# Expert results scattered into token order, read back as plain blocks, with the expert weight loads on another queue

## The chip, the cores and the metric

The kernel runs on one core of a Trainium2 chip. The metric is the time of one execution on the device, in microseconds (us). Five engines run their own instruction streams and meet through semaphores: TensorE (PE; PEld is its weight load), VectorE (DVE), ScalarE (ACT), GpSimd (POOL), and SyncE (SP), which here only issues DMAs. PEq, POOLq and so on are the sequencers of the engines. ACT and POOL can issue DMAs too.

## What is computed

Two transformer layers on x of shape 4 x 1024 x 256, in float32. Layer 0 adds causal attention and a dense feed-forward to x. Layer 1 adds a gated attention and a mixture of 8 experts, both on the same normalized rows:

```python
xn = _layernorm(x, axis=-1)
x = x + _L0_attn_ref(xn, ...) + _L0_ffn_ref(xn, ...)
xn = _layernorm(x, axis=-1)
x = x + _L1_attn_ref(xn, ...) + _L1_ffn_ref(xn, ...)

# _L1_ffn_ref, with E = 8 experts, K = 2 per token
scores = jax.nn.softmax(xf @ Wg.T, axis=-1)
expert_weights, expert_indices = jax.lax.top_k(scores, K)
expert_weights = expert_weights / expert_weights.sum(-1, keepdims=True)
gates = (jax.nn.one_hot(expert_indices, E) * expert_weights[..., None]).sum(axis=1)
g = jax.nn.silu(_lora_in(xf, W1, b1, A1, B1)) * _lora_in(xf, W3, b3, A3, B3)
y_e = _lora_out(g, W2, b2, A2, B2)
y = jnp.einsum('te,ted->td', gates, y_e)
```

## The kernel before

The program has four stages, and each engine runs through them in a fixed order written out as lists of units (`LAYER0_UNITS`, `ATTENTION_UNITS`, `TURN`, and `experts_order`). Near a stage's end a few units of the next one are put in between (`AHEAD`). In this text a unit is named by its letters and number.

Stage 0 (to about 480 us) is layer 0 for all four batches. It also folds the low-rank parts into the expert weights and writes these to DRAM, and it routes. For each token and each of its two choices, POOL writes a row of 257 floats (the normalized token and its gate) to a slot of `slot_rows_scratch` with an indirect DMA (`SC`, line 576, 64 of them). The slots of one expert lie together, so that 71 tiles of 128 rows are left, each of one expert.

Stage 1 (to about 592 us) is layer 1's attention for the first two batches. DVE computes the tables of tiles and experts here (`TB:0` to `TB:6`), and with `TB:7` (nine instructions) the row at which each token's two results will stand (`result_rows`). POOL loads the first expert in the unit `LE`.

Stage 2 (about 592 to 945 us) is the experts: 71 turns of 4.9 us, one for a tile. In turn j the units on PE and DVE are `MA(j+2)`, `MG(j+1)`, `MR(j+3)`, `MC(j+2)`, `MO(j)`. `MR` transposes the rows of a tile, `MA` and `MC` multiply them by two matrices, `MG` transposes the gated product and `MO` multiplies it by the third matrix. ACT does `MG(j+1)`, `MR(j+3)` (copies from PSUM, line 2130) and `MA(j+2)`, which is the SiLU (line 2143). DVE makes `slots_g` from the SiLU's output (line 2182), which `MG` on PE waits for, and the results `ys_ring` (line 2190, a ring of 4). SP's unit `MT(j)` waits for the results of tile j, then loads the slot rows of tile j+6 into `xs_ring` (line 2011, a ring of 6) and stores the results in slot order, as a plain block (line 2012). POOL loads the weights of experts 1 to 7: `ME` (two of three parts and their bias, when the last hidden products of the expert that had the ring slot are read) and `MB` (the third, later). `MU` on SP, at turn 12, loads the rows that stage 3 starts with.

Stage 3 (from 945 us) is the attention for the last two batches. Its results, and those of the first half, are added up in SBUF. To each of 32 tiles of 128 tokens POOL adds the two expert results: 64 indirect DMAs that gather 128 rows and add them (`GX0`, `GX1` for the second half, `GZ0`, `GZ1` for the first; line 1485). Between them POOL computes `rsy`, the power -0.5 of the variances (`YS`, line 1495), for which the final rows (`YF`, lines 1849 and 1857) wait on DVE. SP stores the finished blocks: `SZ` for the first half (line 1473), `SX` for the second (line 1454, and tile by tile at the end, line 1451).

`QK` of stage 3 on ACT writes `q` and `r` (lines 1715 to 1717), which lie in the same memory as `xs_ring`.

## Time and profile before

| | us |
|---|---|
| median of 3 runs | 1084.84 (1083.53 to 1085.21) |
| the profiled execution, its own time | 1088.44 |
| its span, first to last instruction | 1086.8 |
| PE busy | 1044.9 (96%) |
| DVE busy | 798.4 (73%) |
| POOL busy | 432.9 (40%) |
| ACT busy | 393.8 (36%) |
| mean granted clock of PE | 0.981 of full speed |

Busy times are the durations of an engine's instructions. Matmuls overlap in the pipeline, and their ends are modelled. A time from issue to landing is that from the start of a DMA's instruction to the last packet's completion.

### The profile page before, as it was taken

Reading aid. Unit: us, or ns where it says so; the run is one execution under the profiler, and the core shown is the slowest. Engines: PE = TensorE matmul, PEld = TensorE weight load, DVE = VectorE, ACT = ScalarE, POOL = GpSimd, SP = SyncE. Lnnn points to the kernel's source line nnn. Section 1 sums busy time; section 2 is a strip of 40 time slices with the busy share of each in tenths; the row PEclk is TensorE's granted clock in tenths of the full one; section 3 lists DMA queues with packets and bytes.
Section 4 is the critical chain, followed back from the end, with each engine's and each line's share of the span. In section 5 each row is a group of like instructions: output and inputs, shape, how many; then the busy total and the mean of one; then the engine's idle time right before and its main releaser. Section 6 shows DMA issues by size and latency. Waiting matters only on the chain.

```text
span 1086.8 us, 20552 instructions
## 1 busy us (share of the span) xinstructions
PE 1044.9 (96%) x6154; PEld 896.6 (83%) x6154; DVE 798.4 (73%) x1842; ACT 393.8 (36%) x794; POOL 432.9 (40%) x408
## 2 busy tenths in 40 slices
PE   5999999999999999989999999999999999999995
PEld 4899888888989798967868788888888888867774
DVE  5667987798788877786866777777777777763745
ACT  2544454445443536352410222232323232352300
POOL 2723666566656565254112110101001000088886
PEclk7999999999999999989999999999999999999998
DMA  8333344544454436331055556424355151265556
GB/s 253 106 114 120 128 163 140 187 147 141 147 176 145 143 113 226 106 101 50 6 159 171 189 179 210 155 97 148 113 180 195 56 197 50 75 140 86 75 101 146
DMA packets 87255, 147.69 MB, mean 136 GB/s; under 512 B 8433, under 2 KB 64625, under 8 KB 87025
## 3 DMA queue, kind: packets, MB, share of 16 engines
q1 hardware_dynamic: 66416, 98.11, 27.8%
q0 software_dynamic: 20736, 48.28, 16.2%
q8 instruction: 57, 0.93, 0.4%
q14 instruction: 46, 0.37, 0.1%
HBM read 88.91 MB, written 57.45 MB: 135 GB/s over the span
## 4 chain that ended last, share of the span: by engine, by line
PE 68%; DVE 14%; POOL 6%; issue 6%; DMA 4%; ACT 1%; DVEq 0%; POOLq 0%; SPq 0%; ACTq 0%
PE wide L2072 19%; PE wide L592 11%; PE bank L592 11%; PE bank L2072 9%; PE wide L1553 3%; PE bank L2097 3%; POOL first_half L1485 3%; DVE hT L1022 2%; PE wide L1646 2%; DMA x_second<-slot_results_scratch,result_rows 2%; POOL x1b L1485 2%; PE bank L2065 1%; PE bank L1622 1%; POOL x_second L1485 1%; PE bank L1553 1%
## 5 line engine op out<-in xcount | busy, mean ns | idle before, releaser
L2130 ACT ACTIVATE gsT<-bank 128x512 fp32r<-128x512 f32 x71 | 42.5, 599 | 243.4 <-PE bank L2097 243.4
L1945 POOL DMA_DIRECT2D expert_ring<-experts_scratch x24 | 17.1, 711 | 253.3 <-DVE slots_h L2179 186.1
L2072 PEld LDWEIGHTS wide<-expert_ring,gsT 128*128 128x128 f32 x852 | 112.1, 189 | 6.6 <-issue 0.3
L2072 PE MATMUL wide<-expert_ring,xsT 128*128 x432 | 115.9, 404 | 0.9 <-DVE xsT L2161 0.8
L2072 PE MATMUL wide<-expert_ring,gsT 128*128 x852 | 114.0, 282 | 0.1
L2072 PE MATMUL bank<-expert_ring,xsT 128*128 x420 | 112.8, 403 | 0.5 <-issue 0.5
L2072 PEld LDWEIGHTS wide<-expert_ring,xsT 128*128 128x128 f32 x432 | 76.1, 188 | 15.1 <-issue 1.8
L563 POOL TENSOR_TENSOR folded_matrix<-fold,folded_matrix 128x512 fp32r<-128x512 f32 x48 | 64.5, 1350 | 59.7 <-ACT folded_matrix L778 59.6
L576 POOL DMA_INDIRECT slot_rows_scratch<-u,slot x64 | 66.5, 1039 | 49.9 <-issue 20.6
L2072 PEld LDWEIGHTS bank<-expert_ring,xsT 128*128 128x128 f32 x420 | 74.0, 188 | 14.1 <-issue 1.1
L592 PE MATMUL bank<-w,hT 128*128 128x264 f32 x480 | 61.5, 285 | 0.5 <-DVE hT L1022 0.5
L592 PEld LDWEIGHTS bank<-w,hT 128*128 128x128 f32 x480 | 59.5, 188 | 0.8 <-issue 0.7
L592 PE MATMUL wide<-xnT,pT 128*128 128x512 f32 (+2 forms) x288 | 58.8, 350 | 0.0
L1485 POOL DMA_INDIRECT x1b<-slot_results_scratch,result_rows x16 | 27.5, 1721 | 73.4 <-DVE x1b L1813 68.9
L1022 DVE TENSOR_TENSOR hT<-hid,hT 128x512 fp32r<-128x512 f32 x64 | 54.7, 861 | 2.5 <-ACT hid L834 2.3
L2161 DVE TENSOR_TENSOR gsT<-bank,gsT 128x512 fp32r<-128x512 f32 x71 | 49.0, 690 | 9.5 <-ACT gsT L2130 1.4
L2182 DVE SCALAR_TENSOR_TENSOR slots_g<-slots_h,xs_ring,slots_h 128x512 f32<-128x512 f32 x71 | 53.4, 752 | 2.5
L1485 POOL DMA_INDIRECT first_half<-slot_results_scratch,result_rows x32 | 51.5, 1610 | 9.3 <-issue 9.0
L2173 DVE TENSOR_TENSOR slots_h<-wide,expert_bias 128x512 f32<-128x512 f32 x36 | 24.9, 692 | 39.5 <-PE wide L2072 39.5
L592 PEld LDWEIGHTS wide<-xnT,pT 128*128 128x128 f32 x288 | 47.9, 188 | 6.5 <-ACT xp L815 0.3
L592 PE MATMUL bank<-xnT,w 128*128 128x512 f32 x192 | 52.5, 417 | 0.0
L592 PE MATMUL wide<-xnT,w 128*128 128x512 f32 x192 | 49.7, 399 | 0.0
(322 smaller groups left out, 2481.9 us busy)
## 6 DMA issues: line engine op xcount, KB each, us to landing
experts_scratch<-folded_matrix SPq DMA_DIRECT2D x24, 1024.0 KB, 5.2
expert_ring<-experts_scratch POOLq DMA_DIRECT2D x24, 1024.0 KB, 5.5
raw<-in_expert_weights SPq DMA_DIRECT2D x24, 512.0 KB, 6.2
xs_ring<-slot_rows_scratch SPq DMA_DIRECT2D x71, 128.5 KB, 2.5
slot_results_scratch<-ys_ring SPq DMA_DIRECT2D x71, 128.0 KB, 2.6
lora<-in_expert_lora SPq DMA_DIRECT2D x24, 288.0 KB, 3.2
u<-in_L_attn_x SPq DMA_DIRECT2D x4, 1024.0 KB, 5.5
expert_bias<-in_expert_bias POOLq DMA_DIRECT2D x8, 512.0 KB, 6.9
```

The source lines that it names most:

```text
L563: tt(fold_part(n, 1), fold[:, n % 2, :], fold_part(n, 0), ALU.subtract).then_inc(matrix_ready, 1)
L576: nc.gpsimd.indirect_dma_start(out=scr["xs"], in_=xb[:, b % 2, t, 0:ROW], in_offset=None, bounds_check=SLOTS - 1, out_offset=bass.Indirect ...
L592: ins = mm(o, stationary(i), moving(j), start=(first and q == 0), stop=(last and q == 2))
L1022: tt(hT[:, 1, n % IC, :], hid[:, n % 2, :], hT[:, 0, n % IC, :], ALU.subtract).then_inc(hid_low, 1)
L1485: nc.gpsimd.indirect_dma_start(out=target, out_offset=None, in_=scr["ys"], in_offset=index(k, tile_at), bounds_check=SLOTS_T * P - 1, comp ...
L1553: ins = mm(o, stationary(i), moving(j), start=(first and k == 0), stop=(last and k == 2))
L2072: ins = mm(o, parts[i], moving, start=(first and q == 0), stop=(last and q == 2))
L2097: ins = tr(T[1][:, c * P:(c + 1) * P], g[:, j % 2, c * P:(c + 1) * P], ident[:])
L2130: return nc.scalar.activation(o, i, ACT.Copy)
L2161: tt(flat[1], bank, flat[0], ALU.subtract).then_inc(taken, 1)
L2173: tt(h1[:, j % 2, :], H[j % 2][0], bias(e, 0, HID), ALU.add).then_inc(h1_ready, 1)
L2182: stt(out=g[:, i, :], in0=h1[:, i, :], scalar=xs[:, j % ROUND, DIM:ROW], in1=h3[:, i, :], op0=ALU.mult, op1=ALU.mult).then_inc(g_ready, 1)
```

## The change

The results of a tile go to DRAM in token order. The slot row gets a second extra column, `PLACE`, with the row in `token_results_scratch` (2 x 4096 rows) to which the result belongs. DVE writes it in stage 0, with one small instruction for each batch and choice. POOL stores each tile's results with an indirect DMA that takes its row numbers from `xs_ring`: 71 of them instead of 71 plain stores by SP. Because `xs_ring` is now read until that store is done, the next rows may be loaded only after its completion; `xs_ring` has 7 places instead of 6. SP loads the rows of the first 7 tiles, ACT those of the other 64, in the new unit `ML(j+5)` between `MR(j+3)` and `MA(j+2)`. It first waits until the results of tile j-2 have been stored. `QK` of stage 3 on ACT waits until all results are stored.

SP loads the experts' weights. `MU` is moved from turn 12 to just behind the arrival of expert 1. Spare slots get an index out of bounds (the float 1.0 read as an integer), so that nothing is written for them.

In stage 3 the sums are made by 16 plain DMAs with addition, each of 4 tiles (512 KB), instead of 64 indirect ones of one tile. `TB:7` and `result_rows` are gone.

```diff
-ROUND = 6
+ROUND = 7
-ROW = DIM + 1
+ROW = DIM + 2
+PLACE = DIM + 1
...
+            def places(k):
+                ts(x[:, :, PLACE].bitcast(I32), keep["token_at"][:], float(k * TOKENS + OF[b] * SEQ), None, ALU.add)
...
+                places(0)
                 nc.vector.reciprocal(x[:, :, DIM], gate1[:]).then_inc(g_step, 1)
...
     "gpsimd": """
-        ZR:0 ZR:1 ZR:2 ZR:3 ZR:4 YS:1 ZR:5 YS:3 ZR:6 YS:5 ZR:7 YS:7 YS:9 LE:0 LE:1 YS:11 LE:2 YS:13 YS:15
+        ZR:0 ZR:1 ZR:2 ZR:3 ZR:4 YS:1 ZR:5 YS:3 ZR:6 YS:5 ZR:7 YS:7 YS:9 YS:11 YS:13 YS:15
     "sync": """
-        LC:0 LC:1 LC:3 LX:0 LC:2 SX:0 CL:0 SX:1 LX:1 SX:2 SX:3
+        LC:0 LC:1 LC:3 LX:0 LC:2 SX:0 CL:0 SX:1 LX:1 LE:0 LE:1 LE:2 SX:2 SX:3
...
-    "sync": "CL:0:1 SX:1:1 LX:1:5 SX:2:4",
+    "sync": "LX:1:7 SX:2:1",
...
     if engine == "sync":
-        first = [("ML", j) for j in range(ROUND)]
-        return first + [u for j in range(SLOTS_T) for u in ([("MU", 0)] if j == 2 * ROUND else []) + [("MT", j)]]
+        loads = [("MB", 0), ("ME", 1), ("MB", 1), ("MU", 0)]
+        return [("ML", j) for j in range(ROUND)] + loads + [u for e in range(2, E) for u in (("ME", e), ("MB", e))]
     if engine == "gpsimd":
-        return [("MB", 0)] + [u for e in range(1, E) for u in (("ME", e), ("MB", e))]
+        return [("MT", j) for j in range(SLOTS_T)]
     if engine == "scalar":
-        every = (("MG", 1), ("MR", 3), ("MA", 2))
+        every = (("MG", 1), ("MR", 3), ("ML", ROUND - 2), ("MA", 2))
...
+        def add_rows(target, k, b, rows_of, name, n):
+            if k:
+                pool.wait_ge(added[name][n], 16)
+            nc.gpsimd.dma_start(out=target, in_=results[k, b][:, rows_of, :], accum_op=ALU.add).then_inc(added[name][n], 16)
...
             elif kind == "QK":
+                if half and n == 0:
+                    before["results_stored"](act)
...
+            kind, j = un
+            pool.wait_ge(y_taken, j + 1)
+            nc.gpsimd.indirect_dma_start(
+                out=scr["ys"], in_=y[:, j % RING, :], in_offset=None, bounds_check=TOPK * TOKENS - 1, oob_is_err=False,
+                out_offset=bass.IndirectOffsetOnAxis(ap=xs[:, j % ROUND, PLACE:ROW].bitcast(I32), axis=0)
+                ).then_inc(y_out[j % RING], 16)
...
+        def next_rows(j):
+            done = j - ROUND
+            act.wait_ge(y_out[done % RING], 16 * (done // RING + 1))
+            row_load(act, j)
```

On ACT, in the middle of stage 2, this is what stands in a turn and the start of the next before. `gsT` is `MG`, `xsT` is `MR`, and `slots_h` is the SiLU of `MA`:

```order
L2130 ACTIVATE gsT<-bank 128x512 [waits gated_transposed]
L2130 ACTIVATE xsT<-bank 128x256 [waits slots_transposed]
L2143 ACTIVATE slots_h_112<-slots_h_112 128x512 [waits h1_biased]
L2130 ACTIVATE gsT<-bank 128x512 [waits gated_transposed]
L2130 ACTIVATE xsT<-bank 128x256 [waits slots_transposed]
```

And in a turn now, on the same engine at the same place; `slots_out2` is the semaphore of a finished store of results, and `TENSOR_LOAD` reads the tile's place from SBUF into a register:

```order
L2126 ACTIVATE gsT<-bank 128x512 [waits gated_transposed]
L2126 ACTIVATE xsT<-bank 128x256 [waits slots_transposed]
L1988 TENSOR_LOAD tile_row [waits slots_out2]
L1988 ISA x2
L1993 ISA
L1993 DMA xs_ring<-slot_rows_scratch 128x258
L2139 ACTIVATE slots_h_111<-slots_h_111 128x512 [waits h1_biased]
```

The load of the slot rows has moved to ACT, and its wait stands between two ACT instructions of the turn.

On ACT, at the start of stage 3, the first instruction on `q` stands like this before:

```order
L1673 ACTIVATE u<-u,r 128x256 [waits l1_u_in]
L1673 ACTIVATE u<-u,r 128x256
L1720 ACTIVATE v_52<-v_52 128x512 [waits attention_g_taken2]
L1715 ACTIVATE q<-bank,cols_79 128x512 [waits attention_g_done]
L1716 ACTIVATE r<-bank,cols_79 64x512
```

And now:

```order
L1676 ACTIVATE u<-u,r 128x256 [waits l1_u_in]
L1676 ACTIVATE u<-u,r 128x256
L1725 ACTIVATE v_52<-v_52 128x512 [waits attention_g_taken2]
L1720 ACTIVATE q<-bank,cols_79 128x512 [waits slots_out3,slots_out2,attention_g_done,slots_out1,slots_out0]
L1721 ACTIVATE r<-bank,cols_79 64x512
```

The order is the same; `q` has four more semaphores to wait for, those of the stores of results.

On SP, where stage 1 goes over into stage 2, this stands before, around a store of the first half's rows (`attention_x_ready` is the semaphore of these rows):

```order
L1996 TENSOR_LOAD tile_row [waits expert_out_taken]
L1996 ISA x2
L2011 ISA
L2011 DMA xs_ring<-slot_rows_scratch 128x257
L2012 DMA slot_results_scratch<-ys_ring 128x256
L1454 DMA x_scratch<-x1b 128x4x256 [waits attention_x_ready]
```

Now it is this (the row loads of 7 tiles stand ahead of the first row; `attention_g_done` is the semaphore of PE's products):

```order
L1930 TENSOR_LOAD rank_expert [waits matrix_out,ranks_ready]
L1930 ISA x2
L1938 ISA
L1938 DMA expert_ring<-experts_scratch 128x2x1024
...
L1462 DMA x_scratch<-x1b 128x4x256 [waits attention_x_ready]
L1462 DMA x_scratch<-x1b 128x4x256 [waits expert_in0_0,expert_in0_1,expert_in0_2,attention_x_ready]
L1930 TENSOR_LOAD rank_expert [waits attention_g_done]
...
L1322 DMA u<-xn_scratch 128x8x256 [waits expert_in1_0,expert_in1_1,expert_in1_2]
```

Where the store of the last rows of the first half stood beside the experts' results before, the load of expert 1 (line 1930 and what follows) now stands behind it on SP, and `MU` (line 1322) behind the arrival of expert 1.

## Rows read from the trace of the kernel before

**Rows 1.** The head of the page.

```profile
span 1086.8 us, 20552 instructions
```

**Rows 2.** Busy time by stretch: length, PE, PEld, DVE, ACT, POOL, PEclk, DMA share, GB/s.

```profile
680.00:720.00 40.00, 40.00 (x248) 35.22 (x247) 29.28 (x49) 11.24 (x24) 3.22 (x5) 1.00 0.45 149
```

**Rows 3.** Timeline of the end: start, length, instruction, [idle before and what ended it].

```profile
1077.80 1.57 POOL L1485 DMA_INDIRECT first_half<-slot_results_scratch,result_rows  x1 [0.30 <-issue]
1078.91 1.21 POOL L1495 TENSOR_TENSOR rsy<-vey,half 128x2 f32<-128x2 f32 x1
1080.15 0.88 DVE L1849 SCALAR_TENSOR_TENSOR y<-y,mvy,ln_w 128x256 f32<-128x256 f32 x2 [1.33 <-POOL rsy L1495]
1080.95 0.88 DVE L1857 SCALAR_TENSOR_TENSOR x_second<-y,rsy,x_second 128x256 f32<-128x256 f32 x2
1081.77 0.37 SPq L1473 DMA_DIRECT2D out_dram<-first_half  x1
```

**Rows 4.** The final stores: length min/median/max in ns, first and last start.

```profile
L1451 SPq DMA_DIRECT2D out_dram<-x_second x4: 452/480/944, 1082.2 to 1084.2; - x4
```

**Rows 5.** Timeline of one turn of stage 2.

```profile
931.65 0.48 DVE L2190 SCALAR_TENSOR_TENSOR ys_ring<-expert_bias,xs_ring,wide 128x256 f32<-128x256 f32 x1
...
933.88 0.38 ACT L2130 ACTIVATE xsT<-bank 128x256 fp32r<-128x256 f32 x1
...
934.14 0.63 ACT L2143 ACTIVATE slots_h<-slots_h 128x512 f32<-128x512 f32 x1
...
935.85 0.75 DVE L2182 SCALAR_TENSOR_TENSOR slots_g<-slots_h,xs_ring,slots_h 128x512 f32<-128x512 f32 x1
...
937.65 0.60 PE L2097 MATMUL bank<-ident,slots_g 128*128 128x128 f32 x4
```

**Rows 6.** SP's row loads, the register read and the first six DMAs.

```profile
L1996 SPq TENSOR_LOAD <-tile_row x71: 263/268/477, 555.7 to 922.3; - x71
```
```profile
L2007 SPq DMA_DIRECT2D xs_ring<-slot_rows_scratch x6: 338/354/360, 556.7 to 572.4; - x6
```

**Rows 7.** Indirect stores of stage 0: releaser, one at 183.5 us, its landing, all landings.

```profile
L1075 DVE COPY u<-second_gate x4: 165/169/1149, 182.5 to 482.5; 128x8 f32<-128x8 f32 x4
```
```profile
L576 POOL DMA_INDIRECT slot_rows_scratch<-u,slot x1: 1049/1049/1049, 183.5 to 183.5; - x1
...
DMA to landing us min/median/max: 6.1/6.1/6.1
```
```profile
DMA to landing us min/median/max: 2.4/2.8/6.6
```

**Rows 8.** SP at the same time.

```profile
180.89 0.55 SPq L483 DMA_DIRECT2D experts_scratch<-folded_matrix  x1
```

**Rows 9.** An expert load, SP's store beside it, and that store's landing.

```profile
637.24 0.70 POOL L1945 DMA_DIRECT2D expert_ring<-experts_scratch  x1 [27.32 <-DVE slots_h L2179]
```
```profile
638.86 0.75 SPq L2012 DMA_DIRECT2D slot_results_scratch<-ys_ring  x1
```
```profile
slot_results_scratch<-ys_ring SPq DMA_DIRECT2D x1, 128.0 KB, 8.2
```

**Rows 10.** Timeline, DVE where stage 1 ends.

```profile
618.88 0.88 DVE L1857 SCALAR_TENSOR_TENSOR x1b<-y,rsy,x1b 128x256 f32<-128x256 f32 x2
```

**Rows 11.** Timeline of the first microseconds of stage 3.

```profile
945.33 0.48 DVE L2190 SCALAR_TENSOR_TENSOR ys_ring<-expert_bias,xs_ring,wide 128x256 f32<-128x256 f32 x1 [0.69 <-PE wide L2072]
...
946.41 0.99 SPq L1463 DMA_DIRECT2D first_half<-x_scratch  x2
...
952.51 0.69 ACT L1715 ACTIVATE q<-bank,cols 128x512 f32<-128x512 f32 x1
...
959.70 0.66 PE L1582 MATMUL bank<-ident,headB 128*128 128x128 f32 x4 [0.87 <-DVE headB L1802]
```

**Rows 12.** A wait of PE in stage 1, and the stretch behind it.

```profile
479.23 0.82 PE L1582 MATMUL bank<-ident,headB 128*128 128x128 f32 x4 [2.02 <-DVE headB L1802]
```
```profile
480.00:482.00 2.00, 2.00 (x10) 1.78 (x9) 1.85 (x4) 1.11 (x2) 0.05 (x1) 0.50 0.19 66
```

More of the change, by code:

```diff
@@ L234, in tile_rooms @@
     keep["bv"], keep["bo"], keep["cols1"] = a.take("bv", [P, H1]), a.take("bo", [P, DIM]), a.take("cols1", [P, 17])
-    keep["result"] = a.take("result_rows", [P, TOPK, TILES], I32)
     a = Room(nc, *chain)
@@ L1074, in unit @@
                 hold(dve, v_held, *rows_moved(b, 0))
+                places(1)
                 nc.vector.tensor_copy(x[:, :, DIM], gate1[:]).then_inc(gates_turned, 1)
@@ L1370, in attention @@
     x1_b = scr["x1"].rearrange("(b t p) d -> b p t d", p=P, t=TPB)
+    results = scr["ys"].rearrange("(k b t p) d -> k b p t d", k=TOPK, p=P, t=TPB)
     def t_use(un):
@@ L1997, in rows_of, with row_load, arrived, loaded @@
         return rows[bass.ds(at, 1)].rearrange("s p d -> (s p) d")
+    def row_load(engine, j):
+        engine.dma_start(xs[:, j % ROUND, :], rows_of(engine, xs_d, j)).then_inc(x_in[j % ROUND], 16)
     def sync(sp):
+        def arrived(e, m):
+            sp.wait_ge(keep["expert_in"][e % 2][m], PARTS_IN[m] * (e // 2 + 1))
+            sp.sem_inc(expert_ready[m], 1)
+        def loaded(e, parts, left=None):
+            of = expert_of_rank(sp, keep, e)
+            if e >= 2:
+                end = sp.value_load(keep["rank_end"][0:1, e - 2:e - 1], min_val=0, max_val=SLOTS_T)
+                sp.wait_ge(left, end)
+            for m in parts:
+                load_expert_part(sp, io, keep, scr, e, m, of)
         def unit(un):
@@ L2005, in unit @@
                     sp.wait_ge(*before["heads_done"])
-                    sp.wait_ge(keep["ranks_ready"], 4)
-                sp.dma_start(xs[:, j % ROUND, :], rows_of(sp, xs_d, j)).then_inc(x_in[j % ROUND], 16)
-            elif kind == "MT":
-                sp.wait_ge(y_taken, j + 1)
-                if j + ROUND < SLOTS_T:
-                    sp.dma_start(xs[:, j % ROUND, :], rows_of(sp, xs_d, j + ROUND)).then_inc(x_in[j % ROUND], 16)
-                sp.dma_start(ys_d[j], y[:, j % RING, :]).then_inc(y_out[j % RING], 16)
+                    sp.wait_ge(keep["ranks_ready"], 3)
+                row_load(sp, j)
+            elif kind == "ME" and j == 1:
+                sp.wait_ge(*before["output_done"])
+                loaded(j, range(3))
+            elif kind == "ME":
+                loaded(j, (0, 1), h_taken)
+            elif kind == "MB":
+                for m in (0, 1):
+                    arrived(j, m)
+                if j >= 2:
+                    loaded(j, (2,), y_taken)
+                arrived(j, 2)
             elif kind == "MU":
@@ L2022, in gpsimd @@
     def gpsimd(pool):
-        def arrived(e, m):
-            pool.wait_ge(keep["expert_in"][e % 2][m], PARTS_IN[m] * (e // 2 + 1))
-            pool.sem_inc(expert_ready[m], 1)
-        def loaded(e, parts, left=None):
-            of = expert_of_rank(pool, keep, e)
-            if e >= 2:
-                end = pool.value_load(keep["rank_end"][0:1, e - 2:e - 1], min_val=0, max_val=SLOTS_T)
-                hold(pool, loader_held, left, end)
-            for m in parts:
-                load_expert_part(pool, io, keep, scr, e, m, of)
-        def unit(un):
-            kind, e = un
-            if kind == "ME" and e == 1:
-                hold(pool, loader_held, *before["output_done"])
-                loaded(e, range(3))
-            elif kind == "ME":
-                loaded(e, (0, 1), h_taken)
-            elif kind == "MB":
-                for m in (0, 1):
-                    arrived(e, m)
-                if e >= 2:
-                    loaded(e, (2,), y_taken)
-                arrived(e, 2)
+        def unit(un):
+            kind, j = un
[4 more added lines that the diff above has]
+                ).then_inc(y_out[j % RING], 16)
         return unit
@@ L2181, in gate @@
             dve.wait_ge(s_ready, s + 1)
-            stt(out=g[:, i, :], in0=h1[:, i, :], scalar=xs[:, j % ROUND, DIM:ROW], in1=h3[:, i, :], op0=ALU.mult, op1=ALU.mult
+            stt(out=g[:, i, :], in0=h1[:, i, :], scalar=xs[:, j % ROUND, DIM:PLACE], in1=h3[:, i, :], op0=ALU.mult, op1=ALU.mult
                 ).then_inc(g_ready, 1)
```

102 lines of the change are left out of this document (41 added, 61 removed).

## The prediction, made before the changed kernel was run

> **What bounds the kernel now.** I read the head of the page first [rows 1]: 1086.8 us from first to last instruction, in an execution that took 1088.44 us. The sum below is a difference in this execution, and I carry it over to the median of the runs, 1084.84 us, unchanged. Then the busy times by stretch. In the middle of the experts' stage PE is busy for all of a stretch of 40 us at full clock [rows 2], and so it is in the five that follow. So stage 2 is PE's, 4.91 us for a tile, and no work taken from SP, POOL or DVE there can shorten it. The change can win only where PE waits or has ended, and it loses wherever it makes PE wait. Last I read the timelines of the seams, where other engines hand over to PE, and of the end.
>
> **The end: what it gains.** The last `rsy` on POOL is shown from 1078.91, but the indirect gather before it runs from 1077.80 to 1079.37, so it can run only from there to 1080.12 and takes about 0.75 us; DVE waited 1.33 us for it [rows 3]. Now no gather stands ahead of it on POOL (the last addition stands ahead of the last three `rsy`), so it ends at about 1079.67: 0.45 us earlier. DVE's last rows are then done at 1081.83 - 0.45 = 1081.4. SP's gain is larger. The store of the first half's last block was issued only at 1081.77, since it waited for that last gather, and the four stores of the second half stood behind it, from 1082.2 to 1084.2 for the last [rows 3, 4]. With the additions done long before, the first stores go out when their rows are ready, and the last one right behind DVE's last instruction, at 1081.4. The end moves from 1084.2 to 1081.4: **-2.8 us**. If `rsy` is no faster it is -2.3; if earlier waits for `rsy` (0.4 us each, of the same kind) go too, -3.6. What hides the 16 larger additions is some 100 us of stage 3 between them and their readers. POOL is less busy than with 64 gathers, and the one block that is needed last is issued between two `rsy` well before its reader.
>
> **Edits with one answer.** `TB:7` goes from DVE in a stretch in which PE doesn't wait: 0. Eight small instructions write the places; one like them takes 0.17 us [rows 7]. One stands ahead of the head that PE waits 2.02 us for [rows 12]: +0.2 at most, and I take **+0.2**. POOL's share of the loads moves to SP, whose issues cost no engine anything. The first expert's loads stand behind 7 row loads on SP, but the six row loads of before had ended at 572.4 [rows 6], and stage 2 begins at 592: 0. One more small constant is loaded at the start: 0.
>
> **The middle: a new wait on ACT.** In a turn ACT copies `xsT` at 933.88 and starts the SiLU at 934.14; DVE makes `slots_g` of it at 935.85, and PE takes that at 937.65 [rows 5]. Between copy and SiLU ACT now waits for the store of the results of two tiles ago, reads a register and issues a DMA. On SP the way from the register read to the DMA is 1.0 us (555.7 to 556.7), and the DMA's issue 0.35 [rows 6]. Without any wait the SiLU thus starts near 935.3 and ends near 936.0, and `slots_g` ends near 936.8, still 0.9 us before PE wants it. So the 64 register reads and issues cost nothing. They use up 1.2 of the 2.1 us of cover, though. What is left decides on the wait. For PE not to wait, `slots_g` must start by 936.65, the SiLU by 935.97, the DMA by 935.55, the register read by 934.5. The results that it waits for are those of two turns before; their instruction ended at 931.65 + 0.48 - 4.91 = 927.2. The store has **7.3 us** from the end of the result instruction to its completion. Behind ACT's wait are queued the SiLU, then the next turn's copies for PE. DVE's `slots_g` waits for it, and PE's `MG` for that.
>
> How long does it take? No indirect store of results is in the trace of before, but two neighbours are. The 64 indirect stores of slot rows are of the same size: 2.4 to 6.6 us from issue, 2.8 as a rule, and POOL starts one about 0.8 us after DVE's releasing instruction (182.5 + 0.17 to 183.5) [rows 7]. So as a rule 3.6 us, and no wait. But the one at 183.5 us took 6.1, while 2 MB of SP's transfers, begun at 180.89, were in flight [rows 7, 8]: 6.9 us after its releaser. The second neighbour is SP's own store. At each change of expert 2.5 MB are loaded, here from 637.24 [rows 9]. The store issued at 638.86 landed 8.2 us later. By the turn of 4.91 us its results were ready at 637.83, so it was done **9.2 us** after them. It is the first of six such switches (experts 2 to 7), and nobody waited for it. Now ACT does. SP reacts half a microsecond faster than POOL and so starts the bulk earlier; I take 8.6 us, and 8.6 - 7.3 = 1.3 us that PE waits. Ends: 3.6 us is no wait, 10.0 (9.2 plus POOL's slower start) is 2.7. For experts 3 to 7 that is 5 x 1.3 = **+6.5 us** (0 to 13.5).
>
> **The opening of stage 2.** Expert 1 now stands on SP behind the store of the first half's last rows, which are ready at 618.88 + 0.88 = 619.8 [rows 10]; before, POOL loaded it some 13 us earlier, when no result store had a reader. So 3.6 MB begin near 620 beside the stores of the first tiles, which ACT waits for. When they have arrived, `MU` adds 3 MB, and expert 2 comes on top of that. 8.2 us was the price of 2.5 MB; with more in flight I take 2.5 us for the first collision and 2 for those with `MU` and expert 2: **+4.5 us** (0 to 9).
>
> **The start of stage 3.** `QK` on ACT ran at 952.51, and the head that comes of it is what PE waited for (0.87 us at 959.70) [rows 11]. So this is a chain with no cover behind it. It now waits for the last store of results. Those are ready at 945.81; SP begins 3 MB of loads at 946.41, POOL's store starts near 946.6 and has its packets ready a microsecond later. At 8.6 us after the results it is done at 954.4, and a little more for 3 MB is 955: **+2.5 us** (0, if it is done in 3.6, to 6).
>
> **The clock.** Behind the wait of 2.02 us the granted clock was 0.50, that is 1.2 of 2.4 GHz, in the next stretch of 2 us [rows 12], which costs 1 us of PE's time there; that row is the first of three alike, so about 3.4 us with the edges. Behind the wait of 0.87 us it was not lowered. My waits of 1.3 us lie between. For the two or three longer ones I take half of one such loss, **+1.7 us** (0 to 7).
>
> **Sum.** -2.8 + 0.2 + 6.5 + 4.5 + 2.5 + 1.7 = +12.6 us, so 1084.84 + 12.6 = **1097.4 us**.
>
> **What the skill says on it.** The Trainium skill, page "DMA: Bandwidth & Descriptors", section "Queues, rings and completion order", says that each DMA engine takes turns between the queues that have work, packet by packet. By that a small store would overtake the bulk of another queue, and the middle term would be 0. The trace speaks against it, in the store of 8.2 us and the indirect one of 6.1. The same section says that a completion is written only after every earlier write of that DMA engine, across its queues, which fits these two.
>
> **Rivals.** First, **no collision counts**: packets of SP's and POOL's queues take turns, the indirect store lands in 3 to 6 us, and ACT never waits past its cover. For it: before, the bulk was on POOL's queue and the small store on SP's, and now it is the other way round. Against it: rows 7, where the bulk was SP's too. Its time is 1084.84 - 2.8 + 0.2 = 1082.2 us, faster. It decides at 7.3 us from result to completion. By the skill's rule of taking turns this is the outcome. I give it 0.22.
>
> Second, **only the seams cost**. The stores at the five later switches end just within their 7.3 us, because SP starts the bulk earlier, and the opening and the start of stage 3 cost 3 us together instead of 7, with no loss of clock. 1084.84 - 2.8 + 0.2 + 3 = 1085.2 us, about the same: 0.12.
>
> The forecast itself, waits on ACT in seven or more places, has 0.66. Its own range is 1089 to 1109, from half of the new waits to most of their upper ends.
>
> **Chances and range.** This measurement can tell 0.2%, 2.2 us. The first rival is faster by 2.6 us, just over that; the second spreads over all three signs, the forecast is slower throughout. Faster 0.21, same 0.10, slower 0.69. The range must reach to the first rival, since leaving out both would leave out 0.34: 1081 to 1109.
>
> **What would show it.** Right, if PE's timeline has a wait of 1 to 2 us on `slots_g` two turns after each change of expert, if the store of results there lands 7 us or more after issue, and if ACT's register read waits for it; if the first `QK` of stage 3 starts later than 7 us after the last results; and if the last stores on SP follow DVE's last rows at once. Wrong, if the stores beside an expert load land in under 6 us, or if PE's busy time stays at 40 in 40 through stage 2. The gain at the end is wrong if the four last stores still start together.

## The result and the profile after

The changed kernel took 1083.45 us in the median of 20 runs (1077.65 to 1085.14), the kernel before 1085.49 (1083.53 to 1089.60) in the 20 runs beside it. The ratio is 0.9964, 95% interval 0.9951 to 0.9978: 3.9 us faster (2.4 to 5.3), where 12.6 us slower had been forecast. The ratio is that of the means; the medians are only 2.0 us apart. As a median the time lies in the range of the prediction; by the ratio, from the 1084.84 us of the forecast, it is 1080.9, at the range's lower edge. Its sign and size are the first rival's (2.6 us faster).

The head of the page of the changed kernel; the busy times answer to the table ahead of the change, the span to [rows 1].

```profile
span 1082.4 us, 20493 instructions
...
PE 1042.8 (96%) x6154; PEld 894.8 (83%) x6154; DVE 791.5 (73%) x1841; ACT 400.1 (37%) x794; POOL 392.6 (36%) x392
```

The program can be cut at two instructions that every version has: the first and the last result of the experts (`ys_ring` on DVE), and the end of PE's last matmul. These two rows give the cuts in the profile of before, and the two under them those of after: `ys_ring`, with min/median/max in ns and first and last start, and PE's last group, with start and length.

```profile
L2190 DVE SCALAR_TENSOR_TENSOR ys_ring<-expert_bias,xs_ring,wide x71: 473/480/482, 607.4 to 945.3; 128x256 f32<-128x256 f32 x71
```
```profile
1067.65 7.07 PE L1646 MATMUL wide<-wo,oT 128*128 128x256 f32 x32
```
```profile
L2192 DVE SCALAR_TENSOR_TENSOR ys_ring<-expert_bias,xs_ring,wide x71: 472/476/483, 605.3 to 942.4; 128x256 f32<-128x256 f32 x71
```
```profile
1067.34 7.07 PE L1649 MATMUL wide<-wo,oT 128*128 128x256 f32 x32
```

With the same cuts in every profile of this study (from the timelines, in us; `end_gathers_first` and the kernel that waits for one tile ago stand in the text):

| kernel | first to last result | to PE's last end | behind it |
|---|---|---|---|
| before | 337.95 | 129.4 | 12.0 |
| before, second profile | 337.95 | 129.4 | 11.9 |
| before_32_bytes | 334.36 | 129.4 | 12.0 |
| end_store_order | 337.89 | 129.4 | 10.8 |
| changed | 337.08 | 132.0 | 7.9 |
| changed, second profile | 336.82 | 130.7 | 7.9 |
| after_64_bytes | 340.24 | 132.1 | 7.9 |
| no_expert_bulk | 335.57 | 130.4 | 7.9 |
| seam3_loads_wait | 336.93 | 129.4 | 7.9 |
| row_load_behind_silu | 335.20 | 132.1 | 7.9 |
| both_mended | 336.01 | 129.4 | 7.9 |
| both_mended_2 | 335.84 | 129.4 | 7.9 |

The three lengths belong to the program far more than to the execution: two executions of before agree within 0.2 us. Two of the changed kernel agree within 0.3 us in the first and the last length and differ by 1.3 us in the middle one. What lies ahead of the first result varies much more: it was 600.9 to 607.4 us on most chips, and 620 to 625 in the last two sets of runs, with and without the change. So the table is the better scale for effects of 1 us, though each row but two is one execution, and the timed ratios tell whether the sum is right. From it, changed minus before is -0.9, +2.6 and -4.1, together -2.4 us, and -3.9 with the second profile of the changed kernel.

**The middle.** PE's busy time stayed full in the stretch of [rows 2]; in the stretch ahead of it, with the first switch of expert, PE lost 0.07 us (length, PE, PEld, DVE, ACT, POOL, PEclk, DMA share, GB/s):

```profile
640.00:680.00 40.00, 39.93 (x248) 34.85 (x248) 29.06 (x50) 12.69 (x25) 7.78 (x8) 1.00 0.57 200
680.00:720.00 40.00, 40.00 (x249) 35.27 (x249) 29.53 (x50) 12.06 (x24) 7.77 (x8) 1.00 0.45 148
```

The new wait does act, but in this execution it reaches PE once by more than 0.1 us. This is the timeline around the loads of expert 1 in the opening of stage 2, and the landing of the store that ACT waits for (issued at 622.3):

```profile
627.63 0.38 ACT L2126 ACTIVATE xsT<-bank 128x256 fp32r<-128x256 f32 x1
630.42 0.34 ACTq L1993 DMA_DIRECT2D xs_ring<-slot_rows_scratch  x1
630.81 0.63 ACT L2139 ACTIVATE slots_h<-slots_h 128x512 f32<-128x512 f32 x1 [2.81 <-issue]
631.55 0.75 DVE L2184 SCALAR_TENSOR_TENSOR slots_g<-slots_h,xs_ring,slots_h 128x512 f32<-128x512 f32 x1 [2.01 <-ACT slots_h L2139]
632.22 0.48 DVE L2192 SCALAR_TENSOR_TENSOR ys_ring<-expert_bias,xs_ring,wide 128x256 f32<-128x256 f32 x1
632.36 0.66 PE L2093 MATMUL bank<-ident,slots_g 128*128 128x128 f32 x4 [0.85 <-DVE slots_g L2184]
```
```profile
DMA to landing us min/median/max: 7.5/7.5/7.5
```

ACT stood still for 2.81 us between the copy and the SiLU, DVE for 2.01, and PE, as the last in the row, for 0.85. The waits for stores over the whole kernel, from the view of waits for ACT (in total, times, longest; "issue" is the row load's wait, register read and issue together), and all landings of the stores:

```profile
ACT slots_h L2139 <- issue: 41.1, 63, 2.8
```
```profile
DMA to landing us min/median/max: 2.1/2.4/7.5
```

A turn without a collision has 0.41 us of this idle time, so the 63 rows hold about 26 us of pure issue; at the switches a row has 0.7 to 2.0 us.

**The start of stage 3.** Against [rows 11]:

```profile
943.64 0.97 POOL L2042 DMA_INDIRECT token_results_scratch<-ys_ring,xs_ring  x1 [0.81 <-DVE ys_ring L2192]
950.57 0.69 ACT L1720 ACTIVATE q<-bank,cols 128x512 f32<-128x512 f32 x1 [0.89 <-PE wide L1556]
951.37 1.41 POOL L1496 DMA_DIRECT2D x1b<-token_results_scratch  x1 [6.76 <-DMA token_results_scratch<-ys_ring,xs_ring]
957.76 0.80 PE L1585 MATMUL bank<-ident,headB 128*128 128x128 f32 x4 [1.89 <-DVE headB L1807]
```
```profile
958.00:960.00 2.00, 2.00 (x8) 1.68 (x7) 2.00 (x4) 1.09 (x2) 1.28 (x1) 0.53 1.01 161
960.00:962.00 2.00, 2.00 (x7) 1.56 (x6) 1.71 (x4) 0.66 (x2) 0.87 (x2) 0.61 0.68 72
```

`q` starts 8.2 us after the last result's start instead of 7.2 (7.7 and 6.7 us after its end). The profile puts its 0.89 us of idle time down to PE's product; POOL's addition, which waits for the same last store, names the true cause. PE waits 1.0 us longer, and behind that wait the granted clock is at 0.53 and 0.61 for 4 us, near the lower of its two levels; in before it stayed at 1.00.

**The end.** Against [rows 3, 4], the last `rsy`, DVE's last rows, and SP's final stores (min/median/max in ns, first and last start):

```profile
1077.58 0.70 POOL L1503 TENSOR_TENSOR rsy<-vey,half 128x2 f32<-128x2 f32 x1 [3.41 <-DVE vey L1850]
1078.31 0.88 DVE L1854 SCALAR_TENSOR_TENSOR y<-y,mvy,ln_w 128x256 f32<-128x256 f32 x2 [0.81 <-POOL rsy L1503]
1079.11 0.88 DVE L1862 SCALAR_TENSOR_TENSOR x_second<-y,rsy,x_second 128x256 f32<-128x256 f32 x2
```
```profile
L1459 SPq DMA_DIRECT2D out_dram<-x_second x4: 332/378/850, 1075.6 to 1080.0; - x4
```

The four stores no longer start together: the first goes out 4.4 us ahead of the last, and the last right behind DVE's last row (1079.99).

### The profile page after: what moved, and what is told of

The parts are those of the page before. It is cut to its first block, busy times and chain, and to the rows that moved or that the text cites. A ratio compares the mean times of both kernels' runs of the same rounds, so it can differ in the third digit from the quotient of the medians.

```text
span 1082.4 us, 20493 instructions
## 1 busy us (share of the span) xinstructions
PE 1042.8 (96%) x6154; PEld 894.8 (83%) x6154; DVE 791.5 (73%) x1841; ACT 400.1 (37%) x794; POOL 392.6 (36%) x392
## 4 chain that ended last, share of the span: by engine, by line
PE 80%; DVE 13%; issue 4%; DMA 1%; ACT 1%; DVEq 0%; POOL 0%; ACTq 0%; POOLq 0%
PE wide L2068 18%; PE wide L593 12%; PE bank L593 11%; PE bank L2068 9%; PE wide L1556 6%; PE wide L1649 3%; PE bank L2093 3%; PE bank L1556 3%; DVE hT L1028 2%; PE bank L1625 2%; PE wide L1638 2%; PE wide L1635 2%; PE bank L2061 1%; PE bank L1649 1%; DVE st L925 1%
## 5 line engine op out<-in xcount | busy, mean ns | idle before, releaser
L2042 POOL DMA_INDIRECT token_results_scratch<-ys_ring,xs_ring x71 | 69.0, 973 | 271.5 <-DVE ys_ring L2192 262.6
L2068 PEld LDWEIGHTS wide<-expert_ring,gsT 128*128 128x128 f32 x852 | 109.8, 188 | 5.8 <-issue 0.3
L2068 PE MATMUL wide<-expert_ring,gsT 128*128 x852 | 111.8, 280 | 0.1
L1503 POOL TENSOR_TENSOR rsy<-vey,half 128x2 f32<-128x2 f32 x16 | 14.1, 879 | 166.4 <-DVE vey L1850 166.4
L2139 ACT ACTIVATE slots_h<-slots_h 128x512 f32<-128x512 f32 x71 | 45.0, 633 | 45.0 <-issue 41.1
L2163 DVE TENSOR_TENSOR gsT<-bank,gsT 128x512 fp32r<-128x512 f32 x71 | 49.1, 692 | 11.5 <-ACT gsT L2126 2.8
L1028 DVE TENSOR_TENSOR hT<-hid,hT 128x512 fp32r<-128x512 f32 x64 | 52.3, 824 | 2.3 <-ACT hid L835 2.3
```

Source lines behind the costliest of these rows:

```text
L1028: tt(hT[:, 1, n % IC, :], hid[:, n % 2, :], hT[:, 0, n % IC, :], ALU.subtract).then_inc(hid_low, 1)
L2042: nc.gpsimd.indirect_dma_start(out=scr["ys"], in_=y[:, j % RING, :], in_offset=None, bounds_check=TOPK * TOKENS - 1, oob_is_err=False, out ...
L2068: ins = mm(o, parts[i], moving, start=(first and q == 0), stop=(last and q == 2))
L2139: nc.scalar.activation(h1[:, j % 2, :], h1[:, j % 2, :], ACT.Silu).then_inc(s_ready, 1)
L2163: tt(flat[1], bank, flat[0], ALU.subtract).then_inc(taken, 1)
```

## The experiments

My forecast (collisions cost 4 us or more in the middle) had fallen with the result. The theories that the runs had to tell apart: the stores beside a load land just inside the budget, and the gain is the end's; or the collisions cost what I said, and something outside my sum paid for them. A first look showed such a thing: where nothing waits, a turn is 4.85 us long in the changed kernel and 4.91 in before, with PE busy throughout in both.

### Is the length of a turn the program's or the execution's?

The kernel before, once more.

> The kernel before, unchanged, for a second profile of it. In the profile of before a turn of stage 2 took 4.907 us, in that of the changed kernel 4.853 where nothing waits. Theory 'change': the turn is shorter because of the change, so here it is 4.907 again. Rival 'execution': the length of a turn differs from execution to execution, and it can be near 4.85 here too. Time: 1.000 of before either way.

Ratio 0.9997 (0.9982 to 1.0012). A turn is 4.907 us again, in a profile whose whole span is 3.8 us shorter (1083.0). So the 4.907 is the program's, and what differs between executions of one program lies ahead of stage 2.

### Addresses or engines?

```diff
-            "count_to": sb("count_to", [P, E]), "iota8": sb("iota8", [P, E]),
+            "count_to": sb("count_to", [P, E]), "iota8": sb("iota8", [P, E]), "pad": sb("pad", [P, TPB]),
```

> The kernel before with one unused array of 32 bytes per partition. All three profiles of kernels with the old engine code have turns of 4.907 us, all three with the new one 4.83 to 4.85 at the end of the stage, and the matmuls on xsT and gsT last 403 and 282 ns against 401 and 279. The change also adds an array of 32 bytes (token_at), which moves gsT, xsT and most other arrays from 0 to 32 modulo 64. Theory 'addresses': this kernel has turns near 4.85 and is 3 to 4 us faster than before, with none of the change. Rival 'engines': the turn is shorter because SP, ACT and POOL do other things now, so it is 4.907 here and the time is that of before within 0.1%.

Ratio 0.9975 (0.9960 to 0.9989). The first row is that of the results, which gives the length of stage 2; then PE's matmuls on `gsT` and `xsT` in 660 to 720 us of before, and of this kernel (count, busy us, mean ns):

```profile
L2190 DVE SCALAR_TENSOR_TENSOR ys_ring<-expert_bias,xs_ring,wide x71: 472/480/482, 607.4 to 941.8; 128x256 f32<-128x256 f32 x71
```
```profile
L2072 PE MATMUL wide<-expert_ring,gsT 128*128 x153 | 20.5, 282 | 0.0
L2072 PE MATMUL bank<-expert_ring,xsT 128*128 x73 | 19.7, 403 | 0.0
```
```profile
L2072 PE MATMUL wide<-expert_ring,gsT 128*128 x154 | 20.3, 280 | 0.0
L2072 PE MATMUL bank<-expert_ring,xsT 128*128 x72 | 19.1, 401 | 0.0
```

An unused array of 32 bytes takes 3.6 us off stage 2 and nothing off the rest. Each matmul is 2 ns shorter. None of the change is in this kernel. The turn is best read at PE, from one start of the matmuls on `slots_g` to that nine turns later, in before and in this kernel:

```profile
741.39 0.60 PE L2097 MATMUL bank<-ident,slots_g 128*128 128x128 f32 x4
...
785.55 0.60 PE L2097 MATMUL bank<-ident,slots_g 128*128 128x128 f32 x4
```
```profile
740.04 0.60 PE L2097 MATMUL bank<-ident,slots_g 128*128 128x128 f32 x4
...
783.70 0.60 PE L2097 MATMUL bank<-ident,slots_g 128*128 128x128 f32 x4
```

That is 4.907 and 4.851 us (the median of the 57 turns behind the ninth result is 4.907 and 4.853). In the changed kernel the new array `token_at`, also 32 bytes, does the same by accident: it moves `gsT`, `xsT` and most other arrays by 32 bytes, while `expert_ring`, which is placed from the end of the memory, stays. Its turn is 4.853 us too, and the distances between the starts of the 30 matmuls of a quiet turn are those of before_32_bytes within 2 ns, where those of before differ from them by up to 14 ns. The counter-test:

> The changed kernel with 32 unused bytes more, so that gsT and xsT lie at 0 modulo 64 again. Theory 'addresses': turns near 4.907 where nothing waits, matmuls on gsT at 282 ns, and 3 to 4 us more than the changed kernel. Rival 'engines': turns as in the changed kernel, 4.85, and no difference.

My expectation failed here. First to last result is 340.2 us, 3.2 more than in the changed kernel, and at first sight that agrees. But the turns where nothing waits are not near 4.907 us, and the mean on `gsT` was 279 ns, not 282. Two starts five turns apart, and two waits of PE:

```profile
763.10 0.60 PE L2093 MATMUL bank<-ident,slots_g 128*128 128x128 f32 x4
...
787.42 0.60 PE L2093 MATMUL bank<-ident,slots_g 128*128 128x128 f32 x4
...
842.46 0.66 PE L2093 MATMUL bank<-ident,slots_g 128*128 128x128 f32 x4 [0.87 <-DVE slots_g L2184]
...
887.23 0.66 PE L2093 MATMUL bank<-ident,slots_g 128*128 128x128 f32 x4 [0.47 <-DVE slots_g L2184]
```

A turn is 4.864 us (median of 57 turns 4.862), 0.009 more than in the changed kernel, which makes some 0.6 us in the stage. Most of the rest are late stores: those issued at 832.5 and 877.6 landed after 7.3 and 7.0 us, and the four turns of PE behind them were 2.5 us too long together. The time speaks against 3 to 4 us as well: 0.9972 (0.9958 to 0.9986) against before, where the changed kernel's ratio and 3.2 us would give 0.9993.

So the forward test stands: 32 bytes make the old code's turn 4.853 us. The rule that I had made of it, by the place modulo 64 bytes, isn't borne out: moved by 64 bytes the changed kernel has 4.862 us, and the kernel before, not moved at all, 4.907. Either the place modulo 64 isn't what counts, or the changed kernel would have short turns at any place. No run has the changed kernel without a move; that it would then have 4.907 us is inferred from the equal distances above, not shown. Which of the moved arrays matters, and in what relation to `expert_ring`, these runs don't tell either.

### What do the expert loads cost the changed kernel?

```diff
-    at = slice(2 * HID * m, 2 * HID * (m + 1))
+    at = slice(2 * HID * m, 2 * HID * m + wide)
...
-                load_expert_part(sp, io, keep, scr, e, m, of)
+                load_expert_part(sp, io, keep, scr, e, m, of, 16 if e >= 2 else 2 * HID)
```

> The changed kernel, but of the weights of experts 2 to 7 only 16 columns of each 1024 are loaded (so these experts compute with stale weights); every DMA, wait and order stays. Theory 'inside its budget': the loads cost the changed kernel next to nothing, so it stays within 0.5 us of it, while the stores at the switches land at 2.4 us instead of 4.8 to 6.7 and the delays of ACT's SiLU there go away. Theory 'paid and offset': the collisions cost several us as I forecast (6.5 for five switches) and something else paid them back: 4 us or more below the changed kernel.

Ratio 0.9927 (0.9903 to 0.9950) to before. From 640 to 900 us the stores of results land so, first in the changed kernel, then here:

```profile
DMA to landing us min/median/max: 2.3/2.4/6.7
```
```profile
DMA to landing us min/median/max: 2.4/2.4/4.5
```

The 4.5 us that are left stand beside the biases, which are still loaded. First to last result is 1.5 us shorter, 1.3 of it behind the eighth result, where the thinned loads are. That is more than the 0.5 of one theory and far less than the 4 of the other. The ratios, measured on different chips, are 4.0 us apart, with wide intervals; the three lengths together give 3.2 us against the first profile of the changed kernel and 1.6 against the second, part of it at the start of stage 3. PE's wait of 0.8 us near 631 stays, because expert 1 and `MU` are loaded in full here.

### What does the start of stage 3 cost?

```diff
-                    sp.wait_ge(*before["rows_out"])
+                    before["results_stored"](sp)
                     before["experts_in"](sp)
```

> The changed kernel, but SP starts the 3 MB of loads for stage 3 only when the last results are stored. Theory: QK's wait there is long because of these loads (the last store landed some 7 us after its issue); now it lands at 2.4, QK starts when its products are ready, PE's wait on headB is 0.9 us instead of 1.9 and the clock is not lowered behind it: 1 to 3 us below the changed kernel. Rival: the wait on headB and the clock behind it are the seam's own, and the loads that come later cost as much: no difference.

Ratio 0.9941 (0.9922 to 0.9961). The last store lands 2.1 us after its issue, not 6.8, and the wait and the clock are those of before (SP's loads, the first `q`, PE's wait):

```profile
941.30 1.02 SPq L1477 DMA_DIRECT2D first_half<-x_scratch  x2
...
944.98 0.68 ACT L1720 ACTIVATE q<-bank,cols 128x512 f32<-128x512 f32 x1
...
952.16 0.66 PE L1585 MATMUL bank<-ident,headB 128*128 128x128 f32 x4 [0.89 <-DVE headB L1807]
```

The way from the last result to PE's last matmul is 129.4 us as in before, 2.6 less than in the changed kernel's first profile and 1.3 less than in its second. So the price of the seam is the 3 MB that SP starts 0.7 us ahead of the last store.

### How much cover has the wait in the middle?

ML behind MA, so that the SiLU never stands behind the row load:

```diff
-        every = (("MG", 1), ("MR", 3), ("ML", ROUND - 2), ("MA", 2))
+        every = (("MG", 1), ("MR", 3), ("MA", 2), ("ML", ROUND - 2))
```

> The changed kernel, but in a turn ACT does ML behind MA, not ahead of it. The SiLU starts right behind the copy again, and ML's wait may last until the copies of the next turn, about 2.7 us more than now. If my budget is the right picture, no SiLU is late: the wait of PE on slots_g early in stage 2 (0.85 us) goes, so do the delays of ACT's SiLU at the switches (up to 2.8 us), and stage 2 from first to last result is 1 to 1.5 us shorter; the time is 0.5 to 1.5 us below the changed kernel. If these delays never reached PE: no difference.

PE's wait on `slots_g` is gone, and first to last result is 1.9 us shorter, 335.2, with one new wait of 0.31 us on `xsT` near 702. The ratio to before is 0.9916 (0.9895 to 0.9937); against the 0.9964 of the changed kernel, measured apart, that is more than the trace explains.

The other way, a wait for the store of one tile ago:

```diff
-        return [(kind, j + ahead) for kind, ahead in units if j + ahead < SLOTS_T and (kind != "ML" or j > 1)]
+        return [(kind, j + ahead) for kind, ahead in units if j + ahead < SLOTS_T and (kind != "ML" or j > 0)]
...
-        every = (("MG", 1), ("MR", 3), ("ML", ROUND - 2), ("MA", 2))
+        every = (("MG", 1), ("MR", 3), ("ML", ROUND - 1), ("MA", 2))
```

> The changed kernel, but ACT waits in each turn for the store of the results of one tile ago instead of two (ML loads one tile further ahead). By my sum the store then has 7.3 - 4.9 = 2.4 us from the end of the result instruction, and its usual way is 0.8 us to the issue and 2.4 to the landing, 3.2 us. So PE waits 0.8 us or more in each of 64 turns: about 50 us slower, turns of 5.7 us, and 3 to 4 us more in the turns with an expert load. If ACT's cover is larger than I worked out (the rest of the ring gives way), the loss is much smaller.

1229.28 us, ratio 1.130: 144 us slower, not 50. The sign and the place were right, the size wasn't. One turn of it without a load in the way:

```profile
997.68 0.75 DVE L2184 SCALAR_TENSOR_TENSOR slots_g<-slots_h,xs_ring,slots_h 128x512 f32<-128x512 f32 x1 [3.82 <-ACT slots_h L2139]
998.35 0.47 DVE L2192 SCALAR_TENSOR_TENSOR ys_ring<-expert_bias,xs_ring,wide 128x256 f32<-128x256 f32 x1
...
999.60 0.97 POOL L2042 DMA_INDIRECT token_results_scratch<-ys_ring,xs_ring  x1 [7.86 <-DVE ys_ring L2192]
...
1002.70 0.34 ACTq L1993 DMA_DIRECT2D xs_ring<-slot_rows_scratch  x1
1003.09 0.63 ACT L2139 ACTIVATE slots_h<-slots_h 128x512 f32<-128x512 f32 x1 [3.04 <-issue]
1003.83 0.75 DVE L2184 SCALAR_TENSOR_TENSOR slots_g<-slots_h,xs_ring,slots_h 128x512 f32<-128x512 f32 x1 [1.92 <-ACT slots_h L2139]
```

On DVE the results `ys_ring` stand right behind `slots_g`. So a late store makes the SiLU late, that makes `slots_g` late, and that makes the next results and their store late: a closed loop, from 998.35 to the next results at 1004.49, whose length of 6.14 us is the turn whenever nothing else is in the way. It holds one landing of 2.1 to 2.4 us and some 4 us of handing over. My per-turn sum (a shift of 0.8 us) had no loop in it. Beside a load turns were up to 11.5 us long, and the mean granted clock was 0.955. With the wait for two tiles ago the same loop has two turns, 9.7 us, and so, by my estimate, closes only at landings above 9.7 - 4.0 = 5.7 us from issue.

### The end alone, in the kernel before

```diff
-        GZ0:14 GX1:15 YS:11 GZ0:15 GZ1:13 YS:13 GZ1:14 GZ1:15 YS:15
+        GZ0:14 GX1:15 GZ0:15 GZ1:13 GZ1:14 GZ1:15 YS:11 YS:13 YS:15
...
-        LX:0 LZ:0 LZ:1 LX:1 SZ:0 SX:0 SZ:1 SX:1 SX:2 SZ:2 SZ:3 SX:3 EN:0
+        LX:0 LZ:0 LZ:1 LX:1 SZ:0 SX:0 SZ:1 SX:1 SX:2 SZ:2 SX:3 SZ:3 EN:0
```

> The kernel before with the end alone mended: the last six gathers stand ahead of the last three rsy on POOL, and SX:3 ahead of SZ:3 on SP. If the change's gain is the end's (my sum had -2.8 us, bounds -2.3 to -3.6), this has it without the rest: PE's last matmul as in before, and 2 to 3.5 us less after it, ratio 0.997 to 0.998. If the gain sits elsewhere (shorter turns, cheaper sums), this is within 0.1% of before.

My expectation failed, and usefully: ratio 1.0063 (1.0043 to 1.0084), and the part behind PE's last matmul is 16.8 us instead of 9 to 10.

```profile
1073.00 0.88 DVE L1849 SCALAR_TENSOR_TENSOR y<-y,mvy,ln_w 128x256 f32<-128x256 f32 x2 [7.07 <-POOL rsy L1495]
```

POOL has little room to make the gathers earlier: it was busy for 84.3 of the 95 us from 965 to 1060 in before. Its two largest groups there are these, and the last row is the same stretch of the changed kernel (count, busy us, mean ns, idle before):

```profile
L1485 POOL DMA_INDIRECT first_half<-slot_results_scratch,result_rows x24 | 38.3, 1596 | 7.1 <-issue 6.8 <-DMA x_second<-slot_results_scratch,result_rows 0.3
L1485 POOL DMA_INDIRECT x_second<-slot_results_scratch,result_rows x13 | 20.7, 1593 | 3.7 <-issue 2.5 <-DMA first_half<-slot_results_scratch,result_rows 0.9 <-DMA x_second<-slot_results_scratch,result_rows 0.3
```
```profile
L1496 POOL DMA_DIRECT2D first_half<-token_results_scratch x6 | 9.6, 1598 | 0.0
```

So this order doesn't give the end's gain: POOL works on gathers until nearly the end, and whatever stands behind them is late. Other orders weren't tried. The other half, SP's order by itself:

> The kernel before, with SX:3 ahead of SZ:3 on SP and nothing else: the part of the end that is SP's. The rows of x_second are stored when they are ready, and the block of first_half that waits for the last gather goes out last, near 0.5 us after DVE's last instruction instead of 2.4 us before the last store's issue. It is four times the size of the last tile, so it lands later after its issue. Theory (my sum): most of the 2.35 us between DVE's last instruction and the last store's issue goes, and the tail behind PE's last matmul is 10 to 11 us instead of 12.0. Rival: the larger store at the very end gives it back: 12 us.

Behind PE's last matmul it is 10.8 us instead of 12.0; ratio 0.9974 (0.9950 to 0.9998). SP's order by itself is worth 1.2 us, less than a third of the end's 4.1.

### Both edits, and the changed kernel again

> The changed kernel, unchanged, for a second profile. If the lengths by stage are properties of the program: 337.1 us from first to last result, 132.0 from there to PE's last matmul, with a wait of 1.9 us on headB and a lowered clock behind it, 8.0 after it. What differs between executions then lies before the first result, at 605.3 us in the first profile. If the clock's fall at the start of stage 3 was an accident of that one execution: 130.3 instead of 132.0.

Ratio 0.9982 (0.9956 to 1.0009). By stages 336.8, 130.7 and 7.9: the second of my two outcomes. PE waited 2.14 us on `headB`, 0.25 more than in the first profile, and yet the granted clock stayed at 1.00 in the next 2 us:

```profile
977.00:979.00 2.00, 1.51 (x9) 1.33 (x10) 2.00 (x4) 1.18 (x3) 0.85 (x1) 1.00 1.20 192
```

It was lowered behind this wait in four of the six profiles that have it (changed, after_64_bytes, row_load_behind_silu, wait_one_tile_ago), and not in the other two (the second of the changed kernel, no_expert_bulk). It costs about 1.5 us: 132.0 to 132.1 against 130.4 to 130.7.

> The changed kernel with the two edits together: ML behind MA on ACT, and SP's loads for stage 3 behind the last store of results. Theory: the profiles show stage 2 from first to last result at 335.2 us with the first edit (337.1 in the changed kernel), the way from the last result to PE's last matmul at 129.4 us with the second (132.0), and the tail at 7.9 in both. The two don't touch, so here it is 335.2 + 129.4 + 7.9, 4.5 us less than the changed kernel on the same chip, ratio to before about 0.992. Rival: the loads of stage 3 that start later, or the later row loads, cost in the sum what each seemed to save; then it is no better than the changed kernel.

Ratio 0.9898 (0.9860 to 0.9937), and on the same chip the changed kernel had 0.9982.

> The kernel with the two edits once more, on another draw of chip and time, since the chip of the last three runs lost some 20 us in stage 0 against the others and its intervals are wide. By stages: 335 to 336 us from first to last result, 129.4 to PE's last matmul, 7.9 behind it, 472.5 to 473.3 together against 479.4 in before and 475.4 to 477.1 in the changed kernel. So 6.1 to 6.9 us below before if nothing ahead of the first result differs: ratio 0.9937 to 0.9944. If the ratio of 0.9898 was more than chance, it is below 0.992 again.

Ratio 0.9935 (0.9910 to 0.9959), as the trace has it. The stages are 335.8, 129.4 and 7.9, 6.3 us below before. Stage 2 is 0.6 to 0.8 us longer in these two than with the first edit alone. This version beats both kernels: it is some 2 to 4 us below the changed one by its stages.

## Why the prediction was wrong

**The end: right in kind, too small.** -2.8 us forecast, -4.1 found (12.0 to 7.9), beyond my bound of -3.6. The SP part came as worked out: 4.97 us from DVE's last end to the end of the span in before, 2.41 now, 2.6 less where I had 2.35. The term that was mis-sized is DVE's. I took 0.45 us for one `rsy`. All three waits shrank, 0.36, 0.40 and 1.33 us to 0, 0 and 0.81, 1.3 us in all, since `rsy` starts as soon as `vey` is there and takes 0.70 us. DVE's last row now ends 5.6 us behind PE's last matmul instead of 7.1; 0.2 us of these 1.5 I can't place.

**Stage 2 at switches and opening: the step that failed.** Forecast +6.5 and +4.5, together +11; found +2.7. Against before_32_bytes, which has the same short turns, the changed kernel loses 1.85 us up to the eighth result and 0.87 in the 63 turns behind it. The budget was right (the 0.9 us that I gave as left of the cover forget 0.25 us of hand-over to PE, which the budget has): the worst store, 7.5 us from issue, was 1.0 us over the 6.5 that my 7.3 leaves from issue, and PE waited 0.85. In after_64_bytes two stores beside later loads were 0.8 and 0.5 us over it, and PE waited 0.87 and 0.47. What failed is the landing that I carried over. From SP's plain store of 8.2 us [rows 9] I took 8.6 us from the result, 7.8 from issue, for POOL's indirect store at each switch. In the changed kernel they landed 4.8 to 6.7 us after issue, at or just inside the budget. This landing, taken 1 to 3 us too long at the switches and too long in the opening, makes 8.3 of the 16.5 us between forecast and result. The indirect store of 6.1 us [rows 7], which I had beside it, would have been the right row: same queue, same kind of instruction, and the same queue beside it. I chose the larger one because it stood at the very place in the program. Between the two kernels three things changed at that place, the queue of the bulk, the queue of the store and its kind, and no run tells which of them shortens the landing. This is one such place, a megabyte of `MU` and the first of expert 2, each issued within a microsecond or two of a store (KB each, median us to landing):

```profile
x1b<-x_scratch SPq DMA_DIRECT2D x1, 1024.0 KB, 10.1
expert_ring<-experts_scratch SPq DMA_DIRECT2D x1, 1024.0 KB, 11.4
...
token_results_scratch<-ys_ring,xs_ring POOLq DMA_INDIRECT x1, 6.6
```

The store issued at 637.7 landed at 644.3, ahead of `x1b`, issued 1.4 us before it, at 646.4. So it overtook bulk of another queue, though it took 4 us longer than alone. In the Trainium skill, page "DMA: Bandwidth & Descriptors", section "Queues, rings and completion order", the rule that an engine takes turns between queues fits this; I had given it too little weight. In sign the rule was right, in size it says too little: the slowing from 2.4 to 6.6 us was nearly the whole budget.

**What wasn't in the sum: -3.6 us by addresses.** It was measured in the old code (before_32_bytes), and the changed kernel has the same turn. It is about as large as the net gain. If the changed kernel would have had the longer turn without it, which no run shows, it would stand between 0.3 us faster and 1.2 us slower than before (-3.9 + 3.6 by the second profile, -2.4 + 3.6 by the first). I had read the diff for instructions and not for where arrays lie.

**Start of stage 3.** Forecast +2.5, found +1.0 to +1.3, the same overlong landing: 6.8 us, not 7.8 and more. The chain without cover was the right picture. `q` started 7.7 us after the end of the last results, not 9.2. My mark of 7 us was a weak one: it was 6.7 in before.

**What was to show it.** Of the marks that I had named, the waits of 1 to 2 us on `slots_g` after each change of expert don't exist in this execution (there is one, of 0.85 us, in the opening; after_64_bytes has two at later switches); a store did land 7 us or more after issue, but at one place; ACT's row load did wait; the last stores do follow DVE's last rows at once. Of the marks against it, stores below 6 us beside a load were there, and PE's 40 in 40.

**The clock.** Forecast +1.7, found 0 to 1.6, at one place only, and not in each execution.

**Places, `TB:7`, first expert's loads, register reads.** No cost can be seen. A turn of the changed kernel is 4.85 us where nothing is loaded, as in before_32_bytes without these reads. Two instructions of DVE per batch are far below what the part ahead of the first result differs by.

**The sum.** End -4.1, stage 2 +2.7, seam +1.3 to +2.6, addresses -3.6: -2.4 to -3.7 us, beside the -3.9 measured (2.4 to 5.3 faster). That the first rival's 2.6 us came near is luck: it had stores that land in 3 to 6 us and an ACT that never waits past its cover, and its gain was the end's alone, where the measured one is the net of four terms. The second rival had the mechanism: stores at the later switches just within their budget, and 3 us for the opening and the start of stage 3 together (found: 1.85 and 1.3, with the clock up to 2.6). Its 1085.2 us missed because neither the addresses nor the rest of the end's gain was in it.

## What to carry to other kernels

A wait that is added off the critical path is judged by the loop that it closes: add up everything from the awaited event round to the same event of a later turn, and compare it with that many turns; here the wait for two tiles ago costs 1 to 2 us and the wait for one tile ago 144 us. Where a landing beside other traffic has to be estimated, look first at a row of the same queue and instruction kind: in this case it was the better guide (6.1 us, found 4.8 to 6.7) than the row from the same place in the program (8.2). And before a gain of a few tenths of a per cent is put down to a change, insert as many unused bytes into the kernel before as the change adds.

## What I had not expected of the hardware

- An unused array of 32 bytes ahead of `gsT` and `xsT` shortens a turn of 30 matmuls from 4.907 to 4.853 us (1.1% of a stage that PE bounds, 3.6 us over 70 turns; four profiles with the old engine code at the one, one at the other). The changed kernel, moved by 32 bytes, has 4.853 us too; moved by 64 it has 4.862, so the place modulo 64 bytes isn't shown to be the rule. Where nothing waits, PE is busy throughout in all of them. Stage 3, whose arrays move too, shows no change (129.4 us for the way from the last result to PE's last matmul).
- The granted clock fell behind a wait of 1.89 us in one execution and stayed at 1.00 behind one of 2.14 us at the same place in another.
- A plain addition DMA of 512 KB keeps POOL for 1.6 us, as long as an indirect one of 128 rows (1598 and 1596 ns above), at a quarter of the number.
